# Four-layer graph network on one core: layer 0's edge stage and node stage joined into one, with the edge lists gathered by four indirect transfers

## The reference, cut to what matters

```
q, k, v = x @ Wq, x @ Wk, x @ Wv              # 8 heads of 32
score = exp(clip(sum(k[src] * q[dst]) / sqrt(32), -5, 5))
out   = segment_sum(v[src] * score, dst) / (segment_sum(score, dst) + 1e-9)
x1    = layernorm(x + out)
```

## Time and profile before

| | |
|---|---|
| median of 3 runs | 5425.84 us (5420.32 to 5433.01) |
| the profiled execution | 5432.66 us |
| its span, first to last instruction | 5430.9 us |
| PE busy, share of the span | 89% |
| DVE busy | 73% |
| ACT busy | 48% |
| POOL busy | 39% |

### The profile page before, as it was taken

One profiled execution on the slowest core, in us unless ns is written; L12 is line 12 of the kernel. 1 busy time (PEld: TensorE's weight loads), 2 busy tenths in 40 slices (PEclk: granted clock), 3 DMA queues, 4 the chain that ended last, 5 costly groups with the idle time before them and its releaser, 6 DMA issues. The chain is left out here.

```text
span 5430.9 us, 97954 instructions
## 1 busy us (share of the span) xinstructions
PE 4854.7 (89%) x22356; PEld 3728.2 (69%) x22356; DVE 3946.8 (73%) x13675; ACT 2585.5 (48%) x6082; POOL 2142.3 (39%) x2171
## 2 busy tenths in 40 slices
PE   6999877778999999999788888888879999788888
PEld 3666544447888888888577777777756666577777
DVE  4333399997888888888389999999965555566666
ACT  2333344444555555555355655655531111355555
POOL 4666400006555555555245555554445555000000
PEclk8999955559999999999799999999989999899999
DMA  4444399983444444444356666666545555567665
GB/s 113 133 133 133 106 291 295 288 266 106 131 135 130 130 135 131 131 134 130 118 164 186 190 185 181 195 179 184 174 136 163 163 164 164 175 214 214 212 207 167
DMA packets 893392, 921.21 MB, mean 170 GB/s; under 512 B 116765, under 2 KB 855444, under 8 KB 893126
## 3 DMA queue, kind: packets, MB, share of 16 engines
q1 hardware_dynamic: 484174, 444.55, 28.2%
q10 hardware_dynamic: 333688, 318.57, 17.2%
q0 software_dynamic: 75264, 155.06, 10.1%
HBM read 632.48 MB, written 337.88 MB: 179 GB/s over the span
## 5 line engine op out<-in xcount | busy, mean ns | idle before, releaser
L1175 POOL DMA_INDIRECT nodes_near_rows<-hh_d,source_row x392 | 397.9, 1015 | 605.0 <-DVE nodes_weighted L1348 529.1
L767 PE MATMUL nodes_agg<-nodes_msg,nodes_hot 128*128 128x264 f32 x784 | 410.0, 678 | 135.8 <-issue 92.6
L846 POOL DMA_INDIRECT nodes_near_rows<-x_d,nodes_cur x392 | 425.7, 1086 | 236.3 <-POOL nodes_cur L841 169.2
L1491 POOL DMA_INDIRECT edges_xg<-x_d,edge_rows x392 | 371.5, 948 | 258.6 <-PE edges_x_ps L1517 176.2
L432 POOL DMA_INDIRECT edges_xg<-in_x,edge_rows x392 | 370.5, 945 | 256.3 <-PE edges_t_ps L448 135.0
L767 PEld LDWEIGHTS nodes_agg<-nodes_msg,nodes_hot 128*128 128x128 f32 x784 | 229.2, 323 | 316.2 <-issue 275.2
L649 ACT ACTIVATE nodes_x<-nodes_outer_rows,nodes_outer_shift,nodes_outer_rstd 128x256 f32<-128x256 f32 x784 | 425.6, 593 | 19.6 <-DVE nodes_outer_shift L642 14.4
L1733 PE MATMUL nodes_agg<-w_s,nodes_xT 128*128 128x256 f32 x1568 | 412.2, 386 | 1.9 <-ACT nodes_xT L1750 1.9
L854 POOL TENSOR_TENSOR nodes_xb<-nodes_xin,row_L_gnn_b 128x512 f32<-128x512 f32 x196 | 248.1, 1266 | 380.6 <-DVE nodes_inner_rows L880 380.4
L959 PE MATMUL nodes_h_ps<-w_h,nodes_x2T 128*128 128x272 f32 x1568 | 392.2, 393 | 6.7 <-ACT nodes_x2T L1036 6.7
L969 PE MATMUL nodes_hid_ps<-nodes_zT,w_a 128*128 128x256 f32 x1568 | 372.4, 381 | 0.7 <-ACT nodes_zT L1045 0.7
(11 more groups left out here) (209 smaller groups left out, 12468.5 us busy)
## 6 DMA issues: line engine op xcount, KB each, us to landing
nodes_xin<-x_d SPq DMA_DIRECT2D x588, 256.0 KB, 3.1
nodes_msg<-msg_d SPq DMA_DIRECT2D x784, 132.0 KB, 3.5
x_d<-nodes_x ACTq DMA_DIRECT2D x392, 256.0 KB, 3.2
hh_d<-nodes_hh ACTq DMA_DIRECT2D x196, 264.0 KB
x_d<-nodes_y ACTq DMA_DIRECT2D x196, 256.0 KB
nodes_hin<-hh_d SPq DMA_DIRECT2D x196, 256.0 KB, 3.8
nodes_xin<-in_x SPq DMA_DIRECT2D x195, 256.0 KB
out<-nodes_y ACTq DMA_DIRECT2D x195, 256.0 KB, 3.2
```

Of the source, the lines that this page charges most:

```text
L767: last = nc.tensor.matmul(agg[ring(u, 2)][:, h, 0:D + H], hot[:, ring(u, 4), h, :], msg[:, r, h, :], start=True, stop=True)
L846: gp.indirect_dma_start(out=near_rows[:, r, h, :], out_offset=None, in_=x1_d, in_offset=bass.IndirectOffsetOnAxis(ap=cur[:, r, h:h + 1], a ...
L1175: gp.indirect_dma_start(out=near_rows[:, u % NR, h, :], out_offset=None, in_=hh_d, in_offset=bass.IndirectOffsetOnAxis(ap=source_row[:, 2 ...
L1491: gp.indirect_dma_start(out=xg[:, c % 8, k, :], out_offset=None, in_=x3_d, in_offset=bass.IndirectOffsetOnAxis(ap=edge_rows[:, c, k:k + 1] ...
```

## The change

The three stages of layer 0 become one, `layer0`. Its step takes two chunks of edges (j = 0 and 1) and one unit of nodes. The units begin `U0 = 5` steps behind the chunks, so that a unit's edges are stored when its windows are loaded; after step 98 no chunks are left and the last 103 units go on alone. Unit u's windows wait until the first 2u+2 chunks are stored. All steps are written out (`run_units`).

- PSUM: `t_ps` and `q_ps` have one bank each instead of two and `kv_ps` two instead of four; `agg` keeps its four.
- The lists: the 392 small copies to `windows` and the stage `turn_windows` go. POOL gathers the lists by four indirect transfers after the gathers of chunk 3, with offsets from a new tile `first_col`, which `prepare` fills with one more transfer; the casting, transposing and turning happen in steps 3 and 4, and one transfer writes `windows` for the later layers.
- The rows of `x` for units below 104 are loaded on SP's queue as before, those of the other 92 units on POOL's, after its gathers.

```diff
+    first_col = keep("first_col", [WB, 4], I32)
...
-    def edges0(sb, ps, sem, sems, block):
...
-    def turn_windows(sb, ps, sem, sems, block):
...
-    def nodes0(sb, ps, sem, sems, block):
+    def layer0(sb, ps, sem, sems, block):
...
+        t_ps, q_ps = ps("t_ps"), ps("q_ps")
+        kv_ps = [ps(f"kv_ps{k}") for k in range(2)]
         agg = [ps(f"agg{k}", 2) for k in range(2)]
...
+        U0 = 5
+        LATE = (EC // 2 + 6) // 8 * 8
...
+                    if c == 4:
+                        for k in range(4):
+                            gp.indirect_dma_start(out=wrow[:, k, :], out_offset=None, in_=edge_pairs[:, :],
+                                                  in_offset=bass.IndirectOffsetOnAxis(ap=first_col[:, k:k + 1], axis=0))\
+                              .then_inc(lists_in, 16)
...
+                for u in range(LATE, UNITS):
+                    load_x(gp, u)
...
+                    chunks = min(2 * u + 2, EC)
+                    for k in range(4):
+                        if chunks > k:
+                            sp.wait_ge(made_out[k], 16 * ((chunks - 1 - k) // 4 + 1))
...
+                            if c >= 1:
+                                pe.wait_ge(copied, c)
...
+                            if c >= 2:
+                                pe.wait_ge(scaled, c - 1)
...
+                            nc.scalar.activation(made[:, r, D:D + H], dots[:, r, :], ACT.Exp, scale=1.0 / norm).then_inc(exped, 1)
...
+                        else:
+                            u = at(U0 + 3)
+                            if u is not None:
+                                norm_root(act, ln, (None, 8, u))
+                run_units(UNITS, U0 + 5, body)
...
     stage(prepare, "prepare")
-    stage(edges0, "edges0")
-    stage(turn_windows, "turn")
-    stage(nodes0, "nodes0")
+    stage(layer0, "layer0")
```

More of the change, by code:

```diff
@@ L404, in by_chunk @@
         return table[0:EPAD, :].rearrange("(c p) w -> p c w", p=P)
-    def edges0(sb, ps, sem, sems, block):
[L407 to L510, removed]
-                        r, b = ring(c, 4), ring(c, 2)
-                        ve.wait_ge(kv_done, num(c) + 1)
-                        ve.wait_ge(q_copied, num(c) + 1)
-                        if had(c, 2):
-                            ve.wait_ge(dotted, num(c) - 1)
-                        nc.vector.tensor_tensor(prod[:, b, :], kv_ps[r][:, 0:D], qs[:, b, :], ALU.mult).then_inc(prodded, 1)
-                    c = at(3)
-                    if c:
-                        ve.wait_ge(dotted, num(c) + 1)
-                        nc.vector.tensor_scalar(dots[:, ring(c, 4), :], dots[:, ring(c, 4), :], -5.0 * norm, 5.0 * norm,
-                                                ALU.max, ALU.min).then_inc(clipped, 1)
-                    c = at(5)
-                    if c:
-                        r = ring(c, 4)
-                        ve.wait_ge(exped, num(c) + 1)
-                        nc.vector.tensor_tensor(msg[:, r, 0:D].rearrange("p (h c) -> p h c", h=H),
-                                                kv_ps[r][:, D:2 * D].rearrange("p (h c) -> p h c", h=H),
-                                                msg[:, r, D:D + H].unsqueeze(2).to_broadcast([P, H, C]), ALU.mult).then_inc(scaled, 1)
-                run_steps(ve, EC, 5, body)
-            @blk.sync
-            def _(sp):
-                first = [None] * 8
-                def window(t):
-                    if ring(t, 8) == 0:
-                        first[:] = eight_firsts(t, 1)
-                    if had(t, 8):
-                        sp.wait_ge(win_out[ring(t, 8)], 16 * turn(t, 8))
-                    sp.dma_start(windows[bass.ds(num(t), 1), :].rearrange("a (e w) -> a e w", w=2),
-                                 edge_pairs[bass.ds(first[ring(t, 8)], P), :].rearrange("(a e) w -> a e w", a=1))\
-                      .then_inc(win_out[ring(t, 8)], 16)
-                run_steps(sp, TILES, 0, lambda at: window(at(0)))
-                for k in range(8):
-                    sp.wait_ge(win_out[k], 16 * (TILES // 8))
@@ L699, in _ @@
                 first = [None] * 8
[L701 to L709 removed]
+                sp.wait_ge(lists_in, 4 * 16)
@@ L772, in _ @@
[L772 to L790 removed]
+                link = chained(ve, d)
```

348 lines of the change are left out of this document (227 added, 121 removed).

## The result

| | before | after |
|---|---|---|
| median | 5423.08 us (5416.23 to 5433.01, 4 runs) | 5248.24 us (5238.92 to 5255.12, 4 runs) |
| ratio, 95% interval | | 0.9675 [0.9652, 0.9698] |
| profiled execution | 5432.66 us, span 5430.9 | 5255.12 us, span 5253.4 |
| ACT busy, share of the span | 48% | 53% |
| PE busy | 89% | 91% |

The change saves 174.8 us, where 164 were forecast: 5248 against a forecast of 5262 and a range of 5234 to 5335. The last scaling of an edge chunk and the last sum of layer 0 are these two rows; the sum starts at 1052.10 instead of 1218.60, so 166.5 us of the gain lie in layer 0.

What follows compares the result with a forecast made beforehand. PE was taken to bound the edges and DVE `nodes0`; joined, 91 steps at 7.2 us, lists 4, units 277 and turn 3 end layer 0 164 us earlier, giving 5262 us on the median's scale, range 5234 to 5335.

Steps and rivals of the forecast that it cites:

- The sum: Layer 0: edges with lists 713.3 us, then units 277 + 3, last sum at 1054.6 instead of 1218.6, 164 us less.
- PE's part of the step: Joint step on PE: two chunks 6.02 plus the unit's product 0.95, sum 6.97 us, bounds 6.97 and 7.15.
- The loop of ACT and DVE: Joint step, from one odd chunk's exponential to the next through ACT and DVE with two table loads: 7.0 us.
- A play of about 0.8: Joint step: 0.8 us between PE's earliest next transposes (3.8) and k and v due (4.8), letting both loops fit, barely.
- rival (a): Joint steps: ACT's loop sets the bound, waits not overlapping; step about 7.9, 64 us more, 5326; chance 0.28.
- The loads: Joint steps on ACT: two table loads of 1.28 us each, 2.56 a step, 182 in 91 steps, without the page's drain.
- rival (b): Joint steps: switches cost more than the loads, a 2.84 us hole each step; step 9.8, time 5499; chance 0.05.
- The lists: Lists made in the steps: 1.6 for PE's transposes plus 2.4 for DVE's chain, 4 us, range 0 to 6; gathers hidden.
- Units alone, loads on POOL: After the last chunk: 103 units at 2.69 us each, 277 us; loading `x` on POOL's queue costs 0.
- The turn: Where chunks end: unit 97's windows wait for the last chunk's store; 3 us, bounds 0 and 8.
- rival (c): Joint steps: the clock falls to the lower level, step about 14 us, 600 us worse, about 5880; chance 0.03.
- (d): Layer 0: units do not overlap the edges because SP's waits bring windows too late; 5410; chance 0.02.

Runs made afterwards that it cites:

- both kernels in which ACT has room: Changed kernel with an identity for layer 0's root, 5221.81 us; changed kernel with DVE's shift moved directly behind the one-hots, 5225.12 us.
- the double switch: Changed kernel with an added 128x1 square root behind `y` in 89 joint steps, adding 178 table loads; 5523.82 us in one run.
- the one-to-one kernel: New version of the changed kernel: one chunk and one unit a step, roots paired, shift early, list gathers spread, `x` on SP; 5188.83 us, ratio 0.9571.

## Why the prediction was right, point by point

**The sum.** Edges and lists: 713.3 forecast from the first transposition on, 772.42 - 60.61 = 711.8 measured. The rest: 280 forecast, 1052.10 - 772.42 = 279.7 measured. The accuracy to 1.5 us is luck, because two errors met. The 91 steps were charged 107.4 us above the edges' own time; 5 at 6.93 and 86 at 7.18 come to some 104, 3 less. The lists cost 2.4 more than charged. Of the 14 us between forecast and median, 11 lie behind layer 0 (last point).

**PE's part of the step: right.** 6.97 was the floor; it is 6.93, in the first steps and in both kernels in which ACT has room. The product holds PE for 0.89, a little under the 0.95 taken.

**The loop of ACT and DVE: right in mechanism, small in size.** Followed it came to 7.0. It is 7.17: `y` starts 2.15 behind the exponential (2.08 in the sum), the second exponential at 3.14 (3.0), the root at 5.56 (5.4). So nearly all of the difference is there by the second exponential: the hand-over from the shift to `y` and the two halves of `y` take a little longer than in the rows of before. The 7.2 that was used added 0.2 for "jitter", a reason that the trace does not show; so that 7.2 fits 7.17 is partly luck.

**"A play of about 0.8": there, but not for what it was used for.** A play lets PE run ahead for a while; it does not make two loops of different length run at the shorter one. The two pairs of rows at 126 and 161 show the play in use: PE's start moved by 0.59 + 0.16 = 0.75 us against ACT's exponential in five steps, four of them by 7.11 - 6.93 = 0.18, and the longer loop set the pace from then on. (The first two of the seven joint steps at 6.93 have no pair of loads.) "PE and ACT wait for each other in turn" is what the copies and transposes above show, at 7.18 and not at the 7.9 of rival (a), whose waits without overlap do not occur.

**The loads: right.** 2.56 a step, no drain and no hole. The earlier trace rows held a hole of 2.84 behind a root, which rival (b) took for the load's; the double switch has four loads a step and nothing of the kind behind them.

**The lists: too cheap.** Forecast 4, with the gathers' delay "hidden by POOL's slack (3.8 of 7) and the chunks ahead". Measured 2.84 + 1.7 + 0.92 for the eight transposes + 0.95 for the product behind DVE's chain = 6.4. The failed step is the slack: it is that of a joint step, while the lists stand in the fill, where POOL issues one gather after the other without a pause. The four gathers delayed the next by 71.54 - 66.49 = 5.05 us, and 2.84 of that reached PE, so POOL was only some 2.2 us ahead. The chain on DVE cost 0.95 where 2.4 were charged, and the eight transposes 0.92 where 1.6 were.

**Units alone, loads on POOL: right. The turn: right in size, for another reason.** 1033.79 - 1031.10 = 2.69 a unit; `x` on POOL cost 0. The turn is 279.7 - 103 x 2.69 = 2.6 against 3, but no unit waited for its windows as the prediction had it:

```profile
764.42 1.05 PE L635 MATMUL layer_agg<-layer_msg,layer_hot 128*128 128x264 f32 x4
...
768.96 0.68 DVE L737 TENSOR_TENSOR layer_mean_msg<-layer_agg,layer_den 128x512 f32<-128x512 f32 x1
769.74 1.13 PE L635 MATMUL layer_agg<-layer_msg,layer_hot 128*128 128x264 f32 x4 [1.22 <-issue]
...
773.71 0.68 DVE L737 TENSOR_TENSOR layer_mean_msg<-layer_agg,layer_den 128x512 f32<-128x512 f32 x1
...
774.49 2.10 PE L635 MATMUL layer_agg<-layer_msg,layer_hot 128*128 128x264 f32 x4 [3.62 <-issue]
```

Each product starts 0.10 behind the end of DVE's division (`mean_msg`), which frees a bank of `agg`, just as in the units alone. DVE is late there because the last chunks' scalings, ahead of it in its order, still wait for ACT's exponentials and their loads (0.90 in the row at 772.00 above). The products go from 7.17 apart over 5.32, 4.75 and 3.64 to 2.69. Unit 97, whose windows need the last chunk, has its product at 783.51, 2.69 behind the one before. Behind the idle time of 3.62 a product takes 2.10, the lower level of the clock.

**The clock: right.** 1.00 in the whole joint stretch, so rival (c) did not come up; nor did (d), for the products of units stood there from 105.79 on.

**The later stages.** From layer 0's last sum to the end of the span it is 4212.3 before and 4201.3 after, 11 us that were held at zero. The other traces, all with the same later code, have 4184.9 to 4202.8 there; the kernel before with only `nodes0` written out has 4194.6. So 18 us of spread occur from run to run, and the kernel before's profiled execution, 9.6 us over its median, lies above it. So the 11 us are within that spread, and no run shows them to be an effect of the change. What makes the spread is open.

## What to carry to other kernels

Where two neighbouring stages are each held by a different engine, joining them puts the work of one into the time that the other leaves empty; add up every engine's work for one unit of each, and choose the ratio of units so that the engines fill together (here one to one, not two to one). Follow the loop through the engine that gained most operations by hand, in its written order, and compare its length with the busiest engine's: the longer one sets the step whatever reserve lies between them, and the first thing to try is the order, since here moving one 0.15 us instruction was worth 23 us and moving two copies ahead of the exponential and its load 102. Slack that is read in the steady part is not there in the fill.

## What the chip showed that was not expected

- Four loads of the activation table a step run with gaps of 0.01 to 0.02 us around them; a change back and forth costs 2.56 us of ACT, and nothing in the joint stretch while ACT's waits have room for it (639.16 us with the 182 loads and without; 5225.12 and 5221.81 us in all, with ranges that overlap).
- The granted clock stayed at 1.00 with PE 90% busy (360.34 of 400 in the one-to-one kernel), was 0.91 at 77%, and after a single hole of 2.67 us in the fill one chunk's k and v took 3.56 instead of 1.88.
- At a share of 0.94 and 298 GB/s the transfers made a step no longer than 4.02 us, where PE's own work is 3.91 and the rest stands behind DVE's scaling.
- Written out, the 12 instructions of DVE for a unit take 2.69 us (2228 in 186 units); in the hardware loop, the unit takes 2.75.
